# Loading the stacked query and key rows: nine transfers per batch against six, with a repeated source

## The reference, cut to what matters

```python
q = (xn @ Wq + bq).reshape(B, S, H, dk).transpose(0, 2, 1, 3)     # H = 8 heads, dk = 16
k = (xn @ Wk + bk).reshape(B, S, H, dk).transpose(0, 2, 1, 3)
scores = jnp.einsum('bhsd,bhtd->bhst', q, k) / jnp.sqrt(jnp.asarray(dk, x.dtype))
p = jax.nn.softmax(scores, axis=-1)
att = jnp.einsum('bhst,bhtd->bhsd', p, v)
```

## Time and profile before

| what | value |
|---|---|
| median of three runs | 792.43 us |
| span of the profiled execution, first to last instruction | 674.4 us |
| median time less the span | 118.0 us |
| PE busy | 601.6 us, 89% |
| DVE busy | 481.1 us, 71% |
| ACT busy | 391.4 us, 58% |
| POOL busy | 330.5 us, 49% |
| moved by DMA | 106.40 MB, mean 158 GB/s |

### The profile page before, as it was taken

How to read it: one execution, slowest core, us unless ns; L and a number is a source line. 1 busy time by engine, 2 the same in 40 slices (tenths; PEclk the granted TensorE clock), 3 DMA queues, 4 the chain that set the end, 5 groups by cost and what they waited for, 6 DMA issues and landing times. The chain is left out here.

```text
span 674.4 us, 11980 instructions
## 1 busy us (share of the span) xinstructions
PE 601.6 (89%) x3825; PEld 379.6 (56%) x3825; DVE 481.1 (71%) x1275; ACT 391.4 (58%) x866; POOL 330.5 (49%) x363
## 2 busy tenths in 40 slices
PE   8978988999999899798989899898999898889974
PEld 5656557988888797674345688332343324523332
DVE  4478876761794439388869734898998873889897
ACT  3444045889666575448778666676756576455510
POOL 5203378065478764704872601557456464064523
PEclk9999999999999999899999989999989998999999
DMA  8200415677789887949396868117411739311021
GB/s 336 116 1 2 141 44 168 213 247 251 249 304 311 283 315 238 285 151 252 119 232 196 167 234 268 40 40 173 70 25 36 170 114 214 102 47 48 17 63 31
DMA packets 47421, 106.40 MB, mean 158 GB/s; under 512 B 7440, under 2 KB 22608, under 8 KB 45824
## 3 DMA queue, kind: packets, MB, share of 16 engines
q1 hardware_dynamic: 41808, 94.82, 47.3%
q0 software_dynamic: 5120, 10.50, 4.9%
q10 hardware_dynamic: 432, 0.34, 0.2%
HBM read 80.26 MB, written 25.17 MB: 156 GB/s over the span
## 5 line engine op out<-in xcount | busy, mean ns | idle before, releaser
L1199 DVE TENSOR_REDUCE mxs<-PS 128x2 f32<-128x1024 f32 x128 | 151.8, 1220 | 46.3 <-PE PS L1539 46.0
L888 ACT ACTIVATE bufa<-PS 128x512 f32<-128x512 f32 x256 | 140.2, 602 | 60.7 <-PE PS L1555 52.7
L847 ACT ACTIVATE bufb<-PS,bufb 128x128 f32<-128x128 f32 x368 | 103.3, 379 | 65.1 <-PE PS L1504 64.5
L1504 PE MATMUL PS<-bufb 128*128 128x128 f32 x736 | 101.3, 286 | 12.4 <-DMA bufb<-in_experts_dram 10.7
L1504 PEld LDWEIGHTS PS<-bufb 128*128 128x128 f32 x736 | 93.0, 198 | 24.4 <-issue 14.2
L1512 PE MATMUL PS<-bufb 128*128 128x128 f32 x736 | 95.9, 278 | 2.2 <-ACT bufb L847 2.1
L1555 PE MATMUL PS<-stk 108*128 108x512 bf16 x256 | 85.2, 390 | 11.0 <-ACT bufa L888 8.4
L691 POOL DMA_INDIRECT slots_in<-bufb x64 | 65.7, 1026 | 55.2 <-DVE bufb L1145 37.0
L1512 PEld LDWEIGHTS PS<-bufb 128*128 128x128 f32 x736 | 89.4, 193 | 5.3 <-ACT bufb L847 3.9
L1539 PE MATMUL PS<-stk 96*128 96x512 bf16 x256 | 79.9, 399 | 11.2 <-DVE mxs L1199 7.3
L702 POOL DMA_INDIRECT bufb<-slots_out,bufb x64 | 61.9, 968 | 37.5 <-issue 26.7
(11 more groups left out here) (292 smaller groups left out, 958.2 us busy)
## 6 DMA issues: line engine op xcount, KB each, us to landing
bufb<-in_experts_dram SPq DMA_DIRECT2D x92, 514.0 KB, 5.1
slots_out<-bufb SPq DMA_DIRECT2D x30, 256.0 KB, 2.9
stk<-split SPq DMA_DIRECT2D x56, 128.0 KB, 8.4
bufb<-slots_in SPq DMA_DIRECT2D x25, 256.0 KB, 4.5
split<-terms SPq DMA_DIRECT2D x8, 768.0 KB, 4.0
slots_in<-hb SPq DMA_DIRECT2D x2, 1536.0 KB, 9.5
stk<-split SPq DMA_DIRECT2D x8, 384.0 KB, 6.9
X<-in_x_dram SPq DMA_DIRECT2D x4, 512.0 KB, 6.5
```

Source lines behind the costliest of these rows:

```text
L847: last = nc.scalar.activation(hs[:, n % HR, fc, :], ps[:, P * fc:P * fc + P], ACT.Gelu_apprx_tanh, bias=ws[:, n % WR, F + fc:F + fc + 1])
L888: nc.scalar.activation(probs[:, i % PR, j, :], psum("s2", i, j), ACT.Exp, scale=DH1 ** -0.5)\
L1199: nc.vector.tensor_reduce(mxs[:, gr % 2, 2 * j:2 * j + 2, h], psum("s1", i, j).rearrange("p (c n) -> p c n", c=2), axis=AX.X, op=ALU.max)\
L1504: last = nc.tensor.matmul(ps[:, P * fc:P * fc + P], ws[:, n % WR, P * fc:P * fc + P], xq[:, q % 2, P * x:P * x + P], start=True, stop=True)
```

## The change

The six blocks of the stacks are put in another order: (q0,k1), (q1,k1), (q0,k0), (q1,k0), (q2,k0), (q0,k2). Blocks with the same k term are now neighbours: two blocks (32 partitions, from partition 0) with k1, three blocks (48 partitions, from partition 32) with k0, and one (16 partitions, from partition 80) with k2. For each such group there is one transfer into `qst` and one into `kst`. The one into `kst` reads the same 128 KB of `split` once for each block of the group: its source has a leading dimension of 3, 1 or 2 copies whose step is zero. There are six transfers per batch, issued in the order 48, 16, 32 partitions, q and k in turn. The bytes written are the same, 768 KB into each stack. The counts that `s_in` is compared with change from 144 to 96 per use. The matmuls read the same 96 partitions.

```diff
@@ -550,7 +550,7 @@
                     if i:
-                        eng.wait_ge(s_in[(i - 1) % 2], 144 * ((i - 1) // 2 + 1))
+                        eng.wait_ge(s_in[(i - 1) % 2], 96 * ((i - 1) // 2 + 1))
                     eng.dma_start(split.rearrange("t j p n -> p t j n"), terms[:, :, :, :]).then_inc(t_out, 16)
@@ -559,11 +559,11 @@
 
                     def rows(t, j0, j1):
                         return split[t, j0:j1].rearrange("j (i h) n -> (j i) h n", h=H1)
-                    for lo, js in ((0, 3), (3, 2), (5, 1)):
-                        eng.dma_start(qst[i % 2][DH1 * lo:DH1 * (lo + js), :, :], rows(0, 0, js)).then_inc(s_in[i % 2], 16)
-                    for at, k in enumerate((0, 0, 0, 1, 1, 2)):
-                        eng.dma_start(kst[i % 2][DH1 * at:DH1 * at + DH1, :, :], rows(1, k, k + 1))\
-                            .then_inc(s_in[i % 2], 16)
+                    for lo, js, k in ((2, 3, 0), (5, 1, 2), (0, 2, 1)):
+                        at = slice(DH1 * lo, DH1 * (lo + js))
+                        eng.dma_start(qst[i % 2][at, :, :], rows(0, 0, js)).then_inc(s_in[i % 2], 16)
+                        same = rows(1, k, k + 1).unsqueeze(0).broadcast_to([js, DH1, H1, S])
+                        eng.dma_start(kst[i % 2][at, :, :], same).then_inc(s_in[i % 2], 16)
@@ -1534,7 +1534,7 @@
                     if h == 0 and j == 0:
-                        pe.wait_ge(s_in[b % 2], 144 * (b // 2 + 1))
+                        pe.wait_ge(s_in[b % 2], 96 * (b // 2 + 1))
```

## The result

The change makes the kernel slower: 822.98 us (median of four runs, 821.35 to 824.55) against 791.89 for the kernel before on the same chip (787.52 to 793.49), a ratio of 1.0463 (95% interval 1.0414 to 1.0512). The direction was forecast, the size was not: 803.5 with a range to 815. The run that the first profile caught lacked pauses of ACT and DVE, up to 13 us long, that the trace lists as "remote" in later profiles, with the change and without it, so its span was 674.4 us where another profile of the same kernel has 777.4; rows of after are therefore set beside that second profile (the experiment `e0_before_again`), and the cause of the pauses was not found.

A forecast was written before the change was run, and what follows sets the result against it. PE bounds the kernel, four of eight stack loads setting its pace. Delays 3.5 + 3.5 + 2.8 + 3.5 + 0.4 = 13.7, less 3.5 taken back, plus 1 for clock: net 11.2 on 792.4, 803.5 us; own range 796 to 812, reaching 789 to 815.

The forecast's parts named there:

- spread out: Rival for the stack loads: sixteen engines share the repeated source, a batch drains some 3 us sooner, 786 us; chance 0.13.
- The hint for it: In the transfer list, plain SP loads with outermost count below sixteen (pattern, bias rows) show no landing time, suggesting fewer engines.
- 312 KB or 319.5 kB [...] At 24.4 GB/s that is 13.1 us: Leading engine's work per stack load: 56 KB shared plus two whole 128 KB copies; load 3.1 to 3.9 us later, 3.5 taken.
- the slow end: Leading engine of a stack load at 9.8 GB/s, 32.6 us; excluded because three engines at 24.4 ask for only 73 GB/s.
- the prediction's own sum for batch 4: Stack landing after the last experts: 455.23 + 1.9 + 1.3 + 13.1 = 471.5 against 468.7, 2.8 us later.
- The four places forecast: PE's waits growing: weights in batches 0 and 3 by 3.5 us each, batch 4's stack 2.8, batch 7's sorted rows 3.5.
- PE's other matmuls hide 3.5: Batches 1 and 6: slack of 3.1 and 3.6 us hides the later stack, but for some 0.4 in batch 1.
- I take half of these two: Weights waits of batches 0 and 3 come early; PE's later idle moments take back half, 3.5 us.
- The half clock: Behind batch 4's longer wait the granted clock may fall to half, up to 1.7 us of PE work; 1 taken.
- the signs named ahead: Stack landing about 15 us, low DMA share, weights waits 6 us or more, batch 4 about 4, six issues about 0.42.
- Issues at no gain: SP's three fewer issues per batch, 0.46 us each, 1.4 per batch, costed at nothing because data still drain.
- Confined and worse: Rival: few engines at 18 GB/s, stack load 8 us later, slack of batches 1, 2, 5, 6 gone, 826 us; chance 0.10.

The follow-up runs named there:

- e0_before_again: The kernel before, no edit, profiled again: 782.5 us, 1.0039 against the kernel before on the same chip.
- e2_interleaved: The change's six transfers with rows interleaved inside each group, 16 channels outermost and copies second: 774.89 us, 0.9927 against the kernel before.
- e4_after_again: The changed kernel, no edit, run again: 821.84 us, 1.0412 against the kernel before.
- e3_triple_alone: The kernel before with only the three k0 blocks as one repeated-source transfer, on partitions 0 to 47, seven transfers: 805.26 us, 1.0318 against before.
- e8_q_triple_unrepeated: The kernel before with `split` rows padded, three q terms in one unrepeated transfer, other blocks one by one, ten transfers: 814.82 us, 1.0436 against before.
- e5_triple_new_place: The changed kernel with the k1 double block by block, only the triple (partitions 32 to 79) repeated: 816.73 us, 1.0343 against the kernel before.
- e9_interleaved_old_places: The interleaved six transfers with groups at partitions 0, 48 and 80, issued in that order: 785.42 us, 1.0068 against the kernel before.
- e10_interleaved_again: The interleaved six transfers at the new places, unchanged, run again on another chip: 777.69 us, 0.9989 against the kernel before.

## Why the prediction was wrong

**The mechanism was right.** The prediction took the reading that a source beginning with 3 or 2 copies runs on three or two engines; the shares of 0.19 and 0.13 show it, and so does the undoing of it in `e2_interleaved`. The rival "spread out" is excluded.

**The hint for it was weak, and the records behind it were sound.** It rested on transfers that show no landing time in the list. In the second profile of the same kernel the list reads

```profile
bufb<-in_experts_dram SPq DMA_DIRECT2D x92, 514.0 KB
...
stk<-split SPq DMA_DIRECT2D x56, 128.0 KB
```

with no landing time for the plain K blocks either, which had 8.4 in the earlier trace rows. So a missing time by itself says nothing about the number of engines: lost records hide times too, as the prediction allowed. The number of completions recorded does say it, where none is lost. For the eight loads of bias rows (8 partitions) the trace holds 72 in both profiles of before, nine a load and not 16. For the stack of batch 4 it holds 144 before, nine times 16, and 96 in `e2_interleaved`, six times 16; in after it holds 71, four times 16 and only 7 for the triple and the double.

**The step that failed is the term "312 KB or 319.5 kB [...] At 24.4 GB/s that is 13.1 us", with the exclusion of the slow end.** Alone, a confined engine runs as assumed: 79/3 = 26 GB/s and 51/2 = 25.5, against 24.4. But the work isn't all done alone. While the other thirteen still move their 57 kB (a sixteenth of the spread transfers), all sixteen move 175 GB/s at a share of 1.07, 10.9 GB/s each: the rate near 9.8 that the prediction had in the earlier trace rows and set aside for the leading engines. They are no faster than the rest in this time, so the sum should have been 57 kB at 10.9, 5.3 us, and then the two own copies, 262 kB at 26, 10.1 us: 15.4 where 13.1 was taken. The trace closes this: from 579 to 584 three engines move 5 x 74 = 370 kB, 123 each, and from 584 to 591 two move 7 x 42 = 294 kB, 147 each; together 270, about the 262 that this sum leaves for an engine with both copies. Put into the prediction's own sum for batch 4, 15.4 gives 18.1 us from the first issue where it had 15.8. Measured are 18.7 against 12.7, 6.0 later where 2.8 was forecast.

**Batch by batch.** PE's timeline in after, with the waits in brackets; the first scores of batch 4 stand in the chain above, behind a wait of 6.43.

```profile
354.16 2.04 PE L1504 MATMUL PS<-bufb 128*128 128x128 f32 x8 [12.64 <-DMA bufb<-in_experts_dram]
...
395.49 1.01 PE L1539 MATMUL PS<-stk 96*128 96x512 bf16 x2 [6.13 <-issue]
...
398.73 0.61 PE L1555 MATMUL PS<-stk 108*128 108x512 bf16 x1
399.66 0.79 PE L1539 MATMUL PS<-stk 96*128 96x512 bf16 x2 [0.32 <-DVE mxs L1199]
...
492.92 2.05 PE L1504 MATMUL PS<-bufb 128*128 128x128 f32 x8 [10.32 <-DMA bufb<-in_experts_dram]
...
664.05 0.60 PE L1555 MATMUL PS<-stk 108*128 108x512 bf16 x2 [0.99 <-issue]
667.28 1.01 PE L1539 MATMUL PS<-stk 96*128 96x512 bf16 x2 [2.62 <-issue]
...
712.08 1.08 PE L1404 MATMUL PS<-identf,bufb 128*128 128x128 f32 x4 [6.74 <-DMA bufb<-slots_in]
```

And of before, second profile:

```profile
336.49 1.13 PE L1504 MATMUL PS<-bufb 128*128 128x128 f32 x8 [3.42 <-DMA bufb<-in_experts_dram]
...
375.60 0.61 PE L1555 MATMUL PS<-stk 108*128 108x512 bf16 x1 [3.70 <-ACT bufa L888]
379.73 1.03 PE L1539 MATMUL PS<-stk 96*128 96x512 bf16 x2 [3.52 <-DVE mxs L1199]
...
467.00 1.65 PE L1504 MATMUL PS<-bufb 128*128 128x128 f32 x8 [2.31 <-DMA bufb<-in_experts_dram]
...
557.48 0.59 PE L1539 MATMUL PS<-stk 96*128 96x512 bf16 x2 [0.41 <-DMA stk<-split]
...
631.28 1.03 PE L1555 MATMUL PS<-stk 108*128 108x512 bf16 x2 [3.09 <-issue]
...
673.79 0.63 PE L1404 MATMUL PS<-identf,bufb 128*128 128x128 f32 x4 [0.67 <-DMA bufb<-slots_in]
```

The last column is the time from a batch's first stack issue to the next batch's (for batch 7 to the end of the span), after less before. It holds whatever was lost or taken back on the way.

| place | forecast, us later | PE's wait | to the next first issue |
|---|---|---|---|
| batch 0, weights | 3.5 | 12.64 - 3.42 = 9.2 | 10.3 |
| batch 1, stack | 0.4 | 6.13 - 0 = 6.1 | -0.8 |
| batch 2, stack | 0 | none | 0.3 |
| batch 3, weights | 3.5 | 10.32 - 2.31 = 8.0 | 9.6 |
| batch 4, stack | 2.8 | 6.43 - 0.41 = 6.0 | 7.4 |
| batch 5, stack | 0 | 0.79 - 0.33 = 0.5 | 0.7 |
| batch 6, stack | 0 | 2.62 - 0 = 2.6 | -3.4 |
| batch 7, rows | 3.5 | 6.74 - 0.67 = 6.1 | 13.2 |
| sum | 13.7 | 38.5 | 37.3 |
| taken back, and half clock | -3.5 + 1 | -12.3 + 11.1 | |
| behind the first stack issue | 11.2 | 37.3 | 37.3 |

The entry -12.3 + 11.1 comes from PE's busy time behind the first stack issue, the first figure after the length of the stretch, first of after and then of before:

```profile
329.40:822.80 493.40, 379.42 (x2090) 185.58 (x2088) 305.80 (x661) 238.95 (x491) 186.89 (x208) 0.88 0.37 107
```

```profile
321.30:777.40 456.10, 368.29 (x2088) 179.51 (x2087) 306.95 (x663) 238.46 (x490) 187.68 (x208) 0.91 0.44 116
```

PE is busy 11.1 us longer and idle 26.2 us longer. The waits listed grew by 38.5, so 12.3 of that came back as other idle time that shrank. That 38.5 and 37.3 are nearly the same is chance.

- The four places forecast were the right ones, and in the last column no other place costs more than 0.7. The profile of `e4_after_again`, set beside the same profile of before, has 10.4, 12.6, 9.0 and 9.5 for batches 0, 3, 4 and 7 and between -0.9 and 0.7 for the others. Only their sizes were too small. In the trace's list of single DMA packets (192 of 8 KB for each load) the last packet ends 22.9 us after the first issue in batch 0, before 13.1, and 20.5 against 10.7 in batch 3: 9.8 later both times, where it is 6.2 later in batch 4 (18.2 against 12.0). Expert weights are issued behind these two loads and keep the other thirteen engines at work, so that the leading ones get hardly any time alone. The share is 0.86 behind batch 0 where it falls to 0.19 in batch 4; that this is why the loss is larger there was not tried by itself.

```profile
329.00:356.00 27.00, 14.36 (x94) 11.65 (x92) 7.53 (x23) 7.28 (x21) 13.85 (x20) 0.80 0.86 235
```

- "PE's other matmuls hide 3.5" of batches 1 and 6 rested on slacks of 3.1 and 3.6. A load that is 6 us later or more uses them up: 6.1 and 2.6 remain. The trace puts these two waits down to "issue", but it is the stack load that ends them: its last 8 KB packet ends at 394.78 and at 666.56, each time 0.7 us before PE starts (in batch 4, where the trace names the stack, 0.55). Yet neither wait costs time in the end. In before, PE stands still for 3.70 and 3.52 us soon after the first scores of batch 1, held up by pauses of ACT and DVE (5.27 and 7.66 us, listed as "remote"). In after the same two (7.34 and 9.21 us there) run beside the wait for the stack, and the two waits behind it are 0 and 0.32. In batch 6 a wait of 3.09 in before stands against 0.99 in after; what hides the rest there was not followed. So the forecast of next to nothing for batch 1 came true by pauses that the first profile didn't have, and not by the slack: that is luck.
- "I take half of these two", 3.5 back from the early waits of batches 0 and 3: of these nothing shows, they cost 10.3 and 9.6. What was taken back, 12.3, lies elsewhere, for the most part behind batches 1 and 6.
- The half clock came as foreseen, but far larger than the 1 us taken. The granted clock is 0.73 from 591.00 to 597.80, behind batch 4's wait, and over the whole span 0.884 against 0.913; behind the first stack issue PE is busy 11.1 us longer. Of these 6.8 lie behind batch 7's first issue, where PE's 488 matmuls take 103.76 us at a clock of 0.90 and in before 96.95 at 0.97. Not all of it need be the change's: ahead of the first stack issue, where both kernels are the same, PE is already busy 4.2 us longer (265.00 against 260.77). On one chip the two kernels differ by 31 and 33 us (822.98 - 791.89, 821.84 - 788.72), so some 5 of the 37.3 may be the chip's.
- Of the signs named ahead, the low share while the load is unfinished and the weights waits above 6 us (12.64 and 10.32) came; the landing "about 15 us" after the first issue and the stack wait of "about 4" were too small.
- Issues at no gain: nothing contradicts it, and there was less to gain. The six of batch 4 take 3.4 us (572.32 to 575.72) where the nine take 4.0 (544.76 to 548.78), since they are not "six issues of about 0.42": the triple takes SP 0.80 us and the double 0.66. The prediction's 0.46 an issue is 0.48 by its own row, 3.8 us for eight.
- "Confined and worse" (826) ended nearest. Its mechanism, 18 GB/s throughout, is not what happens, though a load some 5 to 10 us later is; and the time that it adds for batches 1, 2, 5 and 6 is not lost, so that its number came near is partly luck. What it and the prediction both lacked is that the leading engine has two phases with a rate each, and not one rate.

## What to carry to other kernels

A transfer that replaces several must keep a long outermost dimension: put the 16 rows outside and the 3 copies inside, or the fewer transfers run on three engines and last longer than the many. To price a load that is unevenly shared, follow its slowest engine through the phases, with the shared rate as long as the others still move and the lone rate behind that, and hold the delay against every slack on the way. A wait that grows is not yet time lost: look whether another wait behind it shrinks, by the time from one batch to the next. A DMA share that falls to a small multiple of a sixteenth while something still waits is the sign to look for.

## What was not expected of the hardware

- Where the copies lie counts: three confined engines move 55 to 56 GB/s on partitions 0 to 47 (`e3_triple_alone`, `e8_q_triple_unrepeated`) and 79 to 87 on 32 to 79 (the change, `e5_triple_new_place`). The Trainium skill has a reason ("SBUF — State Buffer", Door 1: The DMA port swizzle): a partition and the one 32 above it share a port, which the blocks at 0 and 32 do and those at 32, 48 and 64 don't. The rows agree, and so does the order of `e9_interleaved_old_places` (1.0068) and `e10_interleaved_again` (0.9989), though no run here takes that cause alone; the order of issue and the chip differ between these runs too.
- Padding between the terms, with nothing read twice, turned a load over sixteen engines into one over three; with the other q blocks one by one this cost 4.4%.
- The one interleaved kernel gave 0.9927, 0.9989 and 0.994 in three comparisons; where this spread comes from was not found.
